# Layer-norm statistics moved from VectorE to accumulating ScalarE passes, with the router and GpSimd's buffers rearranged

## The reference, cut to what matters

```
h = conv_embed(x)                          # [64, 128, 256]: 64 batches of 128 tokens of 256 channels
h = h + mamba(layernorm(h))                # selective scan, inner width 512, 16 states
h = h + moe(layernorm(h))                  # 8 experts, the best 2 of each token
layernorm(x) = (x - mean(x)) / sqrt(var(x) + 1e-5)          # over the 256 channels
mamba: x_in, z = split(x @ W_in); xc = silu(causal_conv(x_in))
       delta, B, C = softplus(...), xc @ W_xproj
       h_t = exp(delta*A) * h_(t-1) + delta*B*xc;  y = sum over 16 states of h*C
       out = ((y + D*xc) * silu(z)) @ W_out
moe:   logits = x @ w_gate; softmax, top 2; out = sum of gate * (silu(x@wg) * (x@wi)) @ wo
```

## Time and profile before

| | |
|---|---|
| median of three runs | 2831.45 us |
| the profiled execution | 2832.74 us, its span 2830.5 us |
| before the first half unit | 96.3 us |
| from one group to the next | 117.1 us |
| expert phase | about 820 us |
| VectorE busy in a group of 117.1 us | 110.3 us |
| TensorE busy in the same | 108.6 us |
| GpSimd busy in the same | 108.0 us |
| ScalarE busy in the same | 79.7 us |

### The profile page before, as it was taken

How to read it: one execution, slowest core, us unless ns; L and a number is a source line. 1 busy time by engine, 2 the same in 40 slices (tenths; PEclk the granted TensorE clock), 3 DMA queues, 4 the chain that set the end, 5 groups by cost and what they waited for, 6 DMA issues and landing times. The chain is left out here.

```text
span 2830.5 us, 29873 instructions
## 1 busy us (share of the span) xinstructions
PE 2577.9 (91%) x7998; PEld 1297.2 (46%) x7999; DVE 1987.6 (70%) x2175; ACT 1468.1 (52%) x2736; POOL 1949.5 (69%) x961
## 2 busy tenths in 40 slices
PE   4789999999999999999999999977599999999999
PEld 2234444344444444444444444433366666666665
DVE  0689999999999999999999999998222222222222
ACT  1665767767667576675766767653122222222222
POOL 1587999999999999999999999997222222222222
PEclk9999999999999999999999999999699999999999
DMA  1321414224142141331413314123322222222221
GB/s 41 136 103 46 147 36 144 102 62 147 36 144 109 55 148 36 144 111 53 148 44 136 118 46 148 58 109 139 120 45 46 43 44 43 45 44 44 45 44 29
DMA packets 125603, 236.14 MB, mean 83 GB/s; under 512 B 46449, under 2 KB 93714, under 8 KB 109122
## 3 DMA queue, kind: packets, MB, share of 16 engines
q1 hardware_dynamic: 98342, 200.56, 20.9%
q0 software_dynamic: 26128, 34.36, 7.1%
q10 hardware_dynamic: 1036, 0.09, 0.0%
HBM read 182.22 MB, written 53.78 MB: 83 GB/s over the span
## 5 line engine op out<-in xcount | busy, mean ns | idle before, releaser
L545 POOL TENSOR_TENSOR arena<-u,arena 128x2048 f32<-128x2048 f32 x255 | 1155.2, 4530 | 102.6 <-DVE psum L1005 41.1
L1005 DVE TENSOR_TENSOR_SCAN psum<-psum,arena 128x1024 f32<-128x1024 f32 x416 | 951.5, 2287 | 76.9 <-ACT psum L790 73.5
L1430 PE MATMUL psum<-hc,ident 128*128 128x512 f32 x1664 | 836.1, 626 | 134.9 <-DVE hc L1039 134.4
L790 ACT ACTIVATE psum<-delta,a_neg 128x508 f32<-128x508 f32 x1024 | 656.7, 674 | 0.7
L631 POOL DMA_INDIRECT out_dram<-hres,tok_id x136 | 211.8, 1557 | 598.7 <-ACT hres L933 549.9
L1430 PEld LDWEIGHTS psum<-hc,ident 128*128 128x128 f32 x1664 | 300.9, 195 | 548.6 <-DVE hc L1039 293.1
L1568 PE MATMUL psum<-arena,xnt 128*128 x1088 | 515.4, 596 | 0.0
L1039 DVE TENSOR_TENSOR hc<-psum,arena 128x1024 f32<-128x1024 f32 x416 | 507.2, 1219 | 7.5
L1298 DVE COPY z<-psum 128x512 f32<-128x512 f32 x136 | 94.1, 692 | 458.4 <-PE psum L1577 458.4
L933 ACT ACTIVATE hres<-psum,tok_w 128x256 f32<-128x256 f32 x136 | 64.5, 474 | 454.4 <-PE psum L1587 447.7
L1587 PE MATMUL psum<-arena,z 128*128 x1088 | 257.1, 379 | 0.9 <-DVE z L1298 0.9
(11 more groups left out here) (175 smaller groups left out, 2666.4 us busy)
## 6 DMA issues: line engine op xcount, KB each, us to landing
arena<-ssm_rows SPq DMA_DIRECT2D x128, 1024.0 KB, 5.3
delta<-expert_rows SPq DMA_DIRECT2D x136, 129.0 KB, 2.1
h_saved_rows<-hnew SPq DMA_DIRECT2D x16, 512.0 KB
hres<-h_saved_rows SPq DMA_DIRECT2D x16, 512.0 KB, 3.7
out_dram<-h SPq DMA_DIRECT2D x16, 512.0 KB, 2.9
draw<-ssm_rows SPq DMA_DIRECT2D x16, 256.0 KB, 3.4
arena<-in_L_ffn_wg_dram SPq DMA_DIRECT2D x8, 512.0 KB
arena<-in_L_ffn_wi_dram SPq DMA_DIRECT2D x8, 512.0 KB
```

The costliest lines, as they stand in the source:

```text
L545: pool.tensor_tensor(dBx[k % 2], rep, b_rep[:, q * QN:(q + 1) * QN, :], ALU.mult).then_inc(dbx_ready, 1)
L790: last = nc.scalar.activation(o, d, ACT.Exp, scale=a_neg[:, c, n:n + 1])
L1005: nc.vector.tensor_tensor_scan(out_, h, src, 0.0, ALU.mult, ALU.add).then_inc(scan_done, 1)
L1430: last = nc.tensor.matmul(yacc[c % 2], ident[:, :], state[:, i, :], start=False, stop=(nth_sum[k] == LAST_SUM[c] and i == 1))
```

## The change

The two statistics leave VectorE. ScalarE's evacuation of hnew is now four passes of 256 columns, each of which also sums its row (`accum_out`); for h2 four more such passes (`total_h2`) write to xn, which nobody reads. A small pass makes minus the mean (`centre`), and four Square passes with that bias sum the squares (`spread_of`). GpSimd's `rsqrt` takes the variance from there, one instruction shorter.

```
+ON_POOL = {12: hres, 15: hnew, 18: yz[:, 2:4], 21: u[:, 0:2], 23: h2, 26: xn}
+DONE_WITH = {21: 12, 22: 15, 23: 18, 26: 21, 27: 23, 28: 26}
-ON_POOL = {13: hnew, 16: hres, 18: hnew, 21: xn, 23: h2, 26: xn}
-DONE_WITH = {16: 13, 19: 16, 22: 18, 23: 21, 26: 23, 29: 26}

 def evac_h(g, m):                                                  # ScalarE
-    nc.scalar.activation(dst, bank_a, ACT.Copy).then_inc(emb_free, 1)
+    for b in (2 * m, 2 * m + 1):
+        last = nc.scalar.activation(hnew[:, b, :], bank_a[:, (b % 2) * C:(b % 2 + 1) * C], ACT.Identity,
+                                    accum_out=total[:, 0, b:b + 1])
+    last.then_inc(emb_free, 1)
+def total_h2(g, m):
+    actq.wait_ge(h2_ready, 2 * g + m + 1)
+    ...
+        last = nc.scalar.activation(xn[:, b, :], h2[:, b, :], ACT.Identity, accum_out=total[:, 1, b:b + 1])
+def centre(g, which):
+    ...
+    nc.scalar.activation(negm[:, which, :], total[:, which, :], ACT.Copy, scale=-1.0 / C)
+def spread_of(g, which, part):
+    ...
+    for b in (2 * part, 2 * part + 1):
+        last = nc.scalar.activation(xn[:, b, :], src[:, b, :], ACT.Square, bias=negm[:, which, b:b + 1],
+                                    accum_out=squares[:, which, b:b + 1])
 def rsqrt(g, which, ready, done):                                  # GpSimd
-    pool.tensor_scalar(veps[:, which, :], mv[:, which, :, 1], EPS, 1.0, ALU.add, ALU.mult)
-    pool.tensor_scalar(negm[:, which, :], mv[:, which, :, 0], -1.0, 1.0, ALU.mult, ALU.mult)
+    pool.tensor_scalar(veps[:, which, :], squares[:, which, :], 1.0 / C, EPS, ALU.mult, ALU.add)
```

More of the change, by code:

```diff
@@ L667, in norm1, with stats @@
+            def stats(g, which):
+                centre(g, which)
+                spread_of(g, which, 0)
+                spread_of(g, which, 1)
             def norm1(g, part):
@@ L851, in step @@
                         softplus_relu(0, k - 2)
[L852 to L855, removed]
+                    if k == 0:
+                        evac_z(g, 2)
+                    if not last and k in (2, 3):
+                        norm1(g + 1, k - 2)
                     if k == 2:
                         evac_z(g, 3)
-                    if k == 9:
+                    if k == 7:
@@ new lines, in step @@
+                        if k in (6, 10, 13, 16):
+                            evac_xi(g + 1, (6, 10, 13, 16).index(k))
+                        if k in (9, 12, 15, 19):
+                            evac_conv(g + 1, 1 - par, (9, 12, 15, 19).index(k))
+                    if not first:
+                        if k == 5:
+                            softplus_relu(g, 2)
+                        if k == 6:
+                            total_h2(g - 1, 0)
+                        if k == 10:
+                            total_h2(g - 1, 1)
+                            centre(g - 1, 1)
+                        if k in (11, 13):
+                            spread_of(g - 1, 1, (k - 11) // 2)
+                        if k == 14:
+                            softplus_relu(g, 3)
+                        if k in (16, 17):
+                            norm2(g - 1, k - 16)
+                        if k in (20, 22):
+                            evac_xn2t(g - 1, (k - 20) // 2)
+                        if k == 25:
@@ L966, in _ @@
             dve.memset(pad_row[:, C:C + 1].bitcast(I32), TOKENS).then_inc(s_set, 1)
-            def stats(which, src):
-                for b in range(GB):
-                    ins = nc.vector.bn_stats(stat[:, which, b, :], src[:, b, :])
-                ins.then_inc(stat_step[which], 1)
-            def aggregate(g, which, ready):
-                dve.wait_ge(stat_step[which], g + 1)
-                for b in range(GB):
-                    ins = nc.vector.bn_aggr(mv[:, which, b, :], stat[:, which, b, :])
-                ins.then_inc(ready, 1)
-            def stats1(g):
-                dve.wait_ge(emb_free, 2 * (g + 1))
-                ahead(dve, pow1, g)
-                stats(0, hnew)
-            def stats2(g):
-                dve.wait_ge(h2_ready, 2 * g + 2)
-                ahead(dve, pow2, g)
-                stats(1, h2)
             def scan(g, k):
@@ L1162, in step @@
                         gate_y(g - 1, NCH - 1)
-                    if k in (11, 19, 27):
-                        gate_y(g, (k - 11) // HC)
+                    if k in (11, 23, 29):
+                        gate_y(g, (11, 23, 29).index(k))
+                    if not second:
+                        if k == 0:
+                            positions(g - 2)
+                        if k == 1:
+                            slots(g - 2)
                     if not first:
@@ L1209, in step @@
-                        if k == 29:
-                            slots_out(g - 1)
-                    if k == 29 and more:
-                        stats1(g + 2)
-            def tail(g):
+                    if not second:
+                        if k == 0:
+                            new_counts(g - 2)
+                            chosen_positions(g - 2)
+                        if k == 1:
+                            slots_out(g - 2)
+            def tail(g):
+                positions(g - 1)
+                new_counts(g - 1)
+                chosen_positions(g - 1)
+                slots(g - 1)
+                slots_out(g - 1)
```

202 lines of the change are left out of this document (104 added, 98 removed).

## The result

The changed kernel takes 2838.6 us (median of 12 runs, 2835.1 to 2840.6), the kernel before beside it 2831.6 (12 runs). The ratio is 1.0023, 95% interval 1.0015 to 1.0030: 7 us slower, where 2819.5 was forecast. The profiled execution has a span of 2834.9 us, against 2830.5 before.

The account below looks back on a forecast made before the run. VectorE, with the least room of three nearly full engines, was taken to bound each group. From the profiled 2832.7 us, -19 for groups, +4 start, +3 tail gave 2821, or 2819.5 at the median; range 2784 to 2856.

Parts of the forecast that it names:

- What leaves VectorE: Bn_stats and bn_aggr of two norms go, 3.2 us a group; VectorE's own work falls from 110.3 to 107.1 us.
- only move: On VectorE, the router's steps, gates and residuals were said to change place only; the router's steps cost what they did.
- New waits: VectorE's waits for late ScalarE or TensorE, place by place in the new order: 8.9 us a group in all.
- Sum of the waits 8.9 against 6.8: Per group, of 3.2 us leaving VectorE 2.1 come back as waits: -1.1, taken as -1.2, or -19 us over 15.5 groups.
- The accumulator: Cost of accum_out on a ScalarE pass: 0.15 us, bounds 0 to 0.28; a pair 1.3 us, ScalarE about 89 a group.
- rival (b): Slower: ScalarE's late pieces bind each group in k = 24 to 31, +1.6 us a group, 2863 us; chance 0.24.
- Rival (c): Square is not in Exp's table, so spread parts bring table loads, 10 us a group, 2962 us; chance 0.04.
- Start and tail: Outside the groups: start +4 us (bounds 2 to 6) from added ScalarE passes, tail +3 (0 to 6) from later scatters.
- the 6.9 us for which the scatters stood: In the tail, the old scatters' wait for issue, set against slots coming some 9 us later.
- Rival (a): ScalarE is never late at the new places, waits stay 6.8 and the 3.2 us are kept: 2789 us; chance 0.22.
- to bound its stretch: Mid-group, GpSimd's eight units take some 54.4 us; without VectorE's waits it would bound there and keep half of them.

Follow-up runs that it names:

- e5: Changed kernel's order and buffers, but both norms' statistics back on VectorE as bn_stats and bn_aggr, evac_h in two plain passes: 2853.01 us, ratio 1.0073 to the kernel before.
- e4: Changed kernel without the statistics' passes, read-outs and squares on ScalarE (mean and variance constant), order and centre passes kept: 2819.18 us, ratio 0.9949 to the kernel before.
- e6: Kernel before with bn_stats and bn_aggr left out, mean and variance set to 1: 2824.76 us, ratio 0.9976 to the kernel before.
- e1: Changed kernel with silu_z one half unit later, at k = 8 instead of 7: 2805.06 us, ratio 0.9906 to the kernel before.
- e3: Changed kernel with silu_z at k = 8 instead of 7 and chunk 1's gate at 24 instead of 23: 2803.01 us, ratio 0.9896 to the kernel before.
- e8: Changed kernel with the edits of e3 and e10 together: 2779.83 us, ratio 0.9816 to the kernel before.
- e10: Changed kernel with TensorE's add_states of 12 and 15 at k = 19 and 21 instead of 21 and 22: 2816.51 us, ratio 0.9945 to the kernel before.
- e2: Changed kernel with chunk 1's gate one half unit later, at k = 24 instead of 23: 2837.05 us, ratio 1.0019 to the kernel before.
- e7: As e3, with the second turn_x ahead of the router on TensorE at k = 23: 2804.00 us, ratio 0.9907 to the kernel before.
- e9: As e8, with the second half of the last convolution at k = 17 instead of 18: 2778.73 us, ratio 0.9812 to the kernel before.

## Why the prediction was wrong

The direction was wrong. In its own steps, a group:

- **What leaves VectorE, 3.2 us.** The starts in e5 against e4 give: period 118.52 - 116.40 = 2.12, waits 6.9 and 7.7, so 2.9 us of work; the kernel before against e6 gives 2.6 in the old order. That was near. But from the old to the new order VectorE's busy time fell by 2.4 only (110.3 to 107.9 in the windows), and its period less waits by 2.0 (111.0 to 109.0). The moved steps cost 0.3 more than before (e4 against e6, 108.7 and 108.4). The gate is one of them: it adds 0.6 behind the short scan 23, and 0.45 between a long scan and its product (k = 11). I had written that they "only move". The last 0.2 (after against e4) come with ScalarE's passes and lie mostly at k = 14; what makes them is open.
- **New waits.** Scan 9: 2.7 forecast, 2.33 measured, and e1 shows its price. Gate: 1.5 and 1.60. Scan 21: 1.6 and 2.12, since evac_conv ahead of silu_x did not shorten it. Scans 17 and 19 gone: 0.24 left. Scans 26 and 27: 1.9, and 1.27 at 25 and 27. Scan 30: 0.8, and 0.77 at 30 and 31. Scans 12 and 13: 0.4 forecast, none there and 0.1 at scan 14. In all 8.9 us of waits were forecast and 8.4 recorded.
- **The step that failed** is the sum of these two, "Sum of the waits 8.9 against 6.8 ... -1.1 us", taken as -1.2 a group and -19 us. It set unlike things against each other. The 8.9 are waits, counted place by place; the 6.8 are room, period less busy time, which before held 0.7 us of small gaps besides 6.2 of waits (the prediction's own 2.8, 2.2 and 1.2 make 6.2, not 6.8). Like for like its figures give a gain of 3.2 - 2.7 = 0.5 us a group and a time near 2830, next to no change. The other term that failed is the work that leaves: 3.2 forecast, 2.0 measured. Against it stand 8.4 - 6.2 = 2.2 us of new waits, and the period is 0.2 longer. By busy time it is the same: 2.4 us less work, and the room grew from 6.9 to 9.5.
- **The accumulator** was taken as 0.15 for a pass, and a pair of passes with it as 1.3 us. total_h2's pair goes from 946.62 to 947.41, 0.79 us, and a Square pair takes about 1.0; the pair of passes with pointer operands in the earlier trace rows took 0.99 without one. No row shows the same pass with and without it. ScalarE stands at 86, not 89 us. This error worked the other way than the others: at 1.3 us a pair the waits would have been longer. It makes rival (b), which decides from 1.6 us for a pair on, wrong in that condition, though the sign was its own. Its other condition, TensorE late behind the router and the late add_states, is there, but not its effect: the waits of scans 24 to 31 are 2.0 us with the gate's 1.6 beside them, and the time is 24 us under its 2863.
- **Rival (c)**: no Square brings a table load; the exps line has 48 loads in both kernels. The Trainium skill, "ScalarE: Activation LUTs", Table sets, left Square open; this trace shows it among Exps without one.
- **Start and tail.** +4 forecast, and -3.3 measured by the second group's first scan (214.0 for 217.3): the first scan starts only 0.7 later for all the passes ahead of it (one execution each; in e1 to e3, e8 and e10, whose edits leave the start alone, it lies anywhere from 96.6 to 99.2). The first group is 4.0 shorter: its waits fell from 13.9 to 11.3, the rest is work; what makes the waits fewer was not tried. Tail +3 forecast, +4.5 measured. Half of the mechanism was as forecast: slots come later, the last scatter begins at 1988.94 and was at 1982.34, and norm2 starts 5.9 later (1994.38 against the earlier trace rows). But the 6.9 us for which the scatters stood, which the forecast took as cover, are still there:

```profile
1975.94 0.97 POOL L579 DMA_INDIRECT expert_rows<-row,slot  x1 [6.82 <-issue]
...
1994.38 2.08 ACT L843 ACTIVATE row<-h,shift,rstd 128x256 f32<-128x256 f32 x4 [13.13 <-DMA expert_rows<-row,slot]
```

- **The cause.** Of the two halves of the change, the statistics on ScalarE gain 14.4 us and the order loses 21 (e5). Two places of the order are shown to cost: silu_z at k = 7 (e1, 33.5 us) and the add_state of 15 at k = 22, in TensorE's crowded stretch, with that of 12 ahead of it at 21 (e10, 22.1 us). Together, and with the gate one half unit later, they are 58.8 us (e8), more than the order's whole loss, so its other moves must gain: 58.8 - 21 = 38 us at most, if prices add. It is less than that, as 0.73 of the 2.33 us at scan 9 is there only with total_h2's passes (e4). Which moves gain was not tried.
- **Rival (a)**, that ScalarE and TensorE would fit at the new places (2789), failed at just these two; e8, in which they do fit, is at 2780.
- **GpSimd** was to bound its stretch once VectorE's waits were gone. In e8 4.0 us of the changed kernel's 8.4 are gone, and no scan waits for it.

## What to carry to other kernels

Where three engines are each busy for 92 to 94% of the period, as here, freed time on the fullest is worth what the next late piece leaves of it: in e6 nothing of 2.6 us in the steady groups. When waits are added up, set waits against waits, and busy time against busy time. Put a table switch (5.9 us here with its pass, the second load and the exps) into the half unit in which the waiting engine has something else to do; one position was worth 33.5 us. When a wait is taken away and comes back one instruction later (e2, e7, e9), look whether one queue releases both, as TensorE's does here; then move work out of that stretch, as e10 does, not within it.

## What the runs showed of the hardware

Summing a row in a ScalarE pass is a second instruction, ACTIVATION_READ_ACCUMULATOR, recorded with 0.19 us. But it starts 0.1 before the pass ends and the next pass 0.1 before it ends, so a 256-column Identity pass with its read-out steps by 947.01 - 946.62 = 0.39 us. A Square pass with a pointer bias steps by 0.49, as the passes with pointers did before without a read-out:

```profile
1979.69 0.49 ACT L701 ACTIVATE xn<-h,negm 128x256 f32<-128x256 f32 x1
1980.09 0.19 ACT L701 ACTIVATION_READ_ACCUMULATOR xn<-h,negm 128x1 f32 x1
1980.18 0.49 ACT L701 ACTIVATE xn<-h,negm 128x256 f32<-128x256 f32 x1
```
